# One VectorE instruction for the tails of two groups, with the fold ahead of it, in a compressed interaction network on one Trainium2 core

## The reference

```
h = inputs                                             # (512, 40, 32)
for i, (W, bias) in enumerate(params):                 # three layers, 200 outputs each
    x = einsum('bhd,bmd->bhmd', h, inputs)             # all pairs of h and the 40 fields
    y = relu(einsum('oi,bid->bod', W, x.reshape(B, -1, D)) + bias)
    if i != 2:  h, direct = split(y, 2, axis=1)        # 100 feed the next layer, 100 are output
    else:       direct = y
    outs.append(direct)
z = concatenate(outs, axis=1).sum(-1)                  # then three dense layers
```

## Time and profile before

| | before |
|---|---|
| median of 3 runs | 2834.54 us (2829.89 to 2837.47) |
| the profiled execution's own time | 2834.67 us |
| its span, first to last instruction | 2832.9 us |
| TensorE busy | 2777.7 us (98%) |
| VectorE busy | 2637.5 us (93%) |
| ScalarE busy | 1501.3 us (53%) |
| GpSimd busy | 845.0 us (30%) |
| mean granted TensorE clock | 0.996 of full |

### The profile page before, as it was taken

The page is one execution under the profiler, slowest core; times in us unless marked ns, Lnnn a source line. Parts: engine busy times, 40 slices in busy tenths (PEclk is TensorE's granted clock), DMA queues, the critical chain, the costliest instruction groups (busy, mean ns, idle before and its releaser), DMA issues.

```text
span 2832.9 us, 53974 instructions
## 1 busy us (share of the span) xinstructions
PE 2777.7 (98%) x18996; PEld 2759.8 (97%) x18996; DVE 2637.5 (93%) x1945; ACT 1501.3 (53%) x1880; POOL 845.0 (30%) x698
## 2 busy tenths in 40 slices
PE   4999999999999999999999999999999999999999
PEld 3999999999999999999999999999999999999997
DVE  5899999999999999999999999999999999999994
ACT  3555555555555555555555555555555555555553
POOL 4432332332332332333333323323323323323100
PEclk9999999999999999999999999999999999999999
DMA  7433433433433333333333334334334334334320
GB/s 196 97 77 78 96 90 75 100 87 76 102 83 80 98 85 82 96 85 84 94 84 88 92 81 93 90 77 96 89 76 98 89 76 101 87 76 102 91 62 18
DMA packets 286069, 249.65 MB, mean 88 GB/s; under 512 B 31247, under 2 KB 284527, under 8 KB 285938
## 3 DMA queue, kind: packets, MB, share of 16 engines
q1 hardware_dynamic: 209462, 195.99, 24.6%
q0 software_dynamic: 65616, 45.43, 12.1%
q10 hardware_dynamic: 10962, 7.87, 1.0%
HBM read 140.74 MB, written 4.20 MB: 51 GB/s over the span
## 4 chain that ended last, share of the span: by engine, by line
PE 93%; DVE 2%; issue 2%; DMA 1%; POOL 1%; SPq 1%; ACT 0%; another core or an unknown queue 0%; ACTq 0%; DVEq 0%
PE acc L805 61%; PE acc L807 28%; PE hid_ps L818 1%; PE z_ps L822 1%; DVE tails L717 1%; POOL gathered L429 1%; DVE product L712 1%; SPq L366 1%; PE acc L868 0%; DMA acc_copy<-acc_copy 0%; DMA raw_weights<-in_w 0%; PE hid_ps L891 0%; DMA gathered<-in_table,rows_all 0%; DVE weights L672 0%; DVE product L710 0%
## 5 line engine op out<-in xcount | busy, mean ns | idle before, releaser
L805 PE MATMUL acc<-weights,heads 126*128 126x400 f32 (+1 forms) x9088 | 2698.8, 365 | 49.6 <-issue 28.8
L807 PE MATMUL acc<-weights,tails 126*128 126x200 f32 (+1 forms) x9088 | 2323.5, 256 | 0.0
L805 PEld LDWEIGHTS acc<-weights,heads 126*128 126x128 f32 (+1 forms) x9088 | 1715.1, 189 | 53.3 <-issue 37.2
L516 ACT ACTIVATE heads<-product 126x1024 fp32r<-126x1024 f32 (+2 forms) x1152 | 1198.6, 1048 | 1037.3 <-PE acc L807 516.8
L807 PEld LDWEIGHTS acc<-weights,tails 126*128 126x128 f32 (+1 forms) x9088 | 1743.2, 192 | 0.0
L717 DVE TENSOR_TENSOR tails<-product,heads 126x1024 fp32r<-126x1024 f32 (+2 forms) x1152 | 1349.2, 1204 | 2.6 <-ACT heads L516 2.6
L712 DVE TENSOR_TENSOR product<-hid_rep,x_rep 126x2048 f32<-126x2048 f32 x510 | 1167.6, 2289 | 107.4 <-PE acc L807 65.6
L437 POOL DMA_DIRECT2D acc_copy<-acc_copy x189 | 236.3, 1250 | 1742.6 <-ACT acc_copy L522 1741.0
L429 POOL DMA_INDIRECT gathered<-in_table,rows_all x320 | 497.4, 1554 | 100.9 <-issue 96.9
L530 ACT ACTIVATE y_relu<-acc_copy 128x400 f32<-128x400 f32 x192 | 102.3, 533 | 210.3 <-DMA acc_copy<-acc_copy 204.9
L522 ACT ACTIVATE acc_copy<-acc 128x800 f32<-128x800 f32 x192 | 158.8, 827 | 16.1 <-PE acc L807 14.0
(11 more groups left out here) (23 smaller groups left out, 85.7 us busy)
## 6 DMA issues: line engine op xcount, KB each, us to landing
x_rep<-x_rows SPq DMA_DIRECT2D x512, 120.0 KB
hid_rep<-hid SPq DMA_DIRECT2D x511, 120.0 KB
x_pairs<-x_rows SPq DMA_DIRECT2D x191, 280.0 KB
acc_copy<-acc_copy POOLq DMA_DIRECT2D x189, 200.0 KB
hid_rep<-hid SPq DMA_DIRECT2D x511, 5.0 KB
x_pairs<-x_rows SPq DMA_DIRECT2D x63, 120.0 KB
raw_weights<-in_w ACTq DMA_DIRECT2D x12, 500.0 KB, 8.0
gathered<-in_table,rows_all POOLq DMA_INDIRECT x320
```

Source lines behind the costliest of these rows:

```text
L516: act.activation(heads[0:rows, ring % HEADS_RING, 0:tiles, :], product[0:rows, ring % PRODUCT_RING, 0:tiles, :], ACT.Copy).then_inc(heads_ ...
L805: nc.tensor.matmul(acc[:, at.parity, c, 0:2 * LAYER], dims(heads[0:rows, ring % HEADS_RING, k, :], c), w, start=(q == 0 and k == 0), stop= ...
L807: last = nc.tensor.matmul(acc[:, at.parity, c, LAYER:2 * LAYER], dims(tails[0:rows, ring % PRODUCT_RING, k, :], c), w[:, 0:LAYER], start=F ...
```

## The change

The tails of a pair of groups become one instruction of 2048 columns (1792 for layer 0), which waits until both heads are made and then reports both groups at once. A fold that stood between the two tails now stands ahead of the one instruction.

```
-            def make_tails(layer, q, g, ring):
-                tiles, rows = group_tiles(layer, q), OPERAND_ROWS[layer]
-                dve.wait_ge(heads_made, g + 1)
-                dve.tensor_tensor(tails[0:rows, ring % PRODUCT_RING, 0:tiles, :],
-                                  product[0:rows, ring % PRODUCT_RING, 0:tiles, :],
-                                  heads[0:rows, ring % HEADS_RING, 0:tiles, :].bitcast(F32),
-                                  ALU.subtract).then_inc(tails_made, 1)
+            def make_tails(layer, g, ring):
+                tiles, rows = TILES0 if layer == 0 else 2 * GROUP, OPERAND_ROWS[layer]
+                pair = slice(ring % PRODUCT_RING, ring % PRODUCT_RING + 2)
+                heads_pair = slice(ring % HEADS_RING, ring % HEADS_RING + 2)
+
+                def flat(x):
+                    return x.rearrange("p a b c -> p (a b) c")[:, 0:tiles, :]
+
+                dve.wait_ge(heads_made, g + 2)
+                dve.tensor_tensor(flat(tails[0:rows, pair, :, :]), flat(product[0:rows, pair, :, :]),
+                                  flat(heads[0:rows, heads_pair, :, :]).bitcast(F32),
+                                  ALU.subtract).then_inc(tails_made, 2)
...
             def make_previous_tails(g, ring, between=None):
 
-                layer, q = previous[0]
-                make_tails(layer, q, g - 2, (ring - 2) % RING)
+                layer = previous[0][0]
                 if between:
                     fold(*between)
-                make_tails(layer, q + 1, g - 1, (ring - 1) % RING)
+                make_tails(layer, g - 2, (ring - 2) % RING)
                 previous[0] = None
```

## The result

The changed kernel takes 2984.93 us (median; 2982.38 to 2989.24), the one before, run beside it, 2835.89: a ratio of 1.0529 (95% interval 1.0514 to 1.0545), 149 us slower. The prediction was 3016 us, in a range of 2950 to 3055: the direction held, the size was 31 us too large, and of the three costs that the prediction added up two came about; the third, the late fold of layer 2, did not. The span is 2982.4 us.

A forecast was written before the change was run, and what follows sets the result against it. TensorE was taken to set the time, VectorE just ahead of it. A turn of 45.63 us against 42.79 gave 170 us over sixty turns, plus 12 for the others: 2834.67 + 182, rounded to 3016 us, range 2950 to 3055.

The forecast's parts named there:

- three costs: The pair loop's stalls, the fold ahead at (1,2) and the fold ahead at (2,4); 2.84 us a turn with restarts.
- the late fold of layer 2: At (1,2): fold waits for a relu ending at 7.69; (1,2) starts at 10.35, with (1,0)'s stall 1.54 us together.
- The loop of 4.83 us against 4.70: VectorE's way round a pair, 0.27 + 2.21 + 2.29 + 0.06 us, exceeds TensorE's time for a pair by 0.13.
- stall at (2,2): (2,2) to (2,4)'s predecessor pair: the plain loop takes 4.83 us against 4.69, 0.14 more.
- The fold of layer 1 ahead of (2,4): Fold waits for its relu, so (2,4) starts 10.72 us after (2,0) against 9.72: 1.00 more.
- (1,4) to stay unstalled: From (1,4) to (1,6), VectorE needs 9.1 us, TensorE's two pairs take 10.10: no stall, only 0.09 of restart.
- The sum: A turn of 45.63 us against 42.79, 2.84 more; 170 us for sixty turns, 12 for others, giving 3016.
- The outer turns: Five turns outside the hardware loop (1, 2, 3, 64, 65): 12 us counted, between 0 and 28.
- The pair loop alone: Rival, chance 0.07: folds wait little as transfers land earlier in longer turns; 1.16 us a turn, 2907 us.
- the 1.6 that the rival had charged to each turn: Clock rival, chance 0.04: TensorE's stalls halve its clock for 3.2 us each turn, some 100 us more, 3116.
- VectorE's saving: Rival "Faster", chance 0.03: if VectorE set the time, fewer, longer instructions would save 31 us: 2803.
- What I said the profile would show: Signs: TensorE waits for tails some 110 us, nearly 190 times; turn 45.6; tails 2.29; 0.7 idle before folds.

The follow-up runs named there:

- E1: The changed kernel with both folds behind the pair's single tails instruction instead of ahead of it: 2918.15 us, ratio 1.0285.
- E3: The changed kernel with a pair's products in two instructions, each waiting only for its own group's place in the ring: 2976.53 us, ratio 1.0492.
- E4: E3 with both folds behind the tails, which stay one instruction: 2854.14 us, ratio 1.0058.
- E7: The changed kernel with a pair's products in two instructions, with the single wait of before ahead of both: 2998.85 us, ratio 1.0573.
- E9: The changed kernel with only the fold of layer 1 behind the tails, that of layer 2 still ahead: 2936.57 us, ratio 1.0367.
- E6: The changed kernel with SyncE's eight hid_rep transfers for layer 2 issued later in the loop, by a later wait: 3021.38 us, ratio 1.0647.
- E2: The kernel before, two tails a pair, with the fold ahead of both tails: 2878.17 us, ratio 1.0137.
- E5: The kernel before, two tails a pair, with both folds behind the two tails: 2843.75 us, ratio 1.0031.

## Why the prediction was right, and where it was off

The direction and two of the three costs came about by the mechanism forecast; the fold of layer 2, which the prediction called the larger term of its two, cost next to nothing in the loop. In a turn 0.73 us too much at (1,2) met 0.25 too little at (1,4) and (2,4), so the time came nearer than the parts were.

- **The loop of 4.83 us against 4.70.** Measured 4.82 at (1,0), (1,4) and (2,0). (1,2) and (2,2) came at 4.80 and 4.79, but TensorE wasn't stopped there: the 0.09 are the restart before. So the 0.14 forecast as a stall at (2,2) was no stall; the loop's start, set at 0.27 us behind TensorE's start of a pair, hangs on the end of the group before, which a stop doesn't delay. E1 shows it without the folds, E3 and E4 remove it by letting the first product start earlier, E7 shows that this permission and not the splitting did it.
- **The fold of layer 1 ahead of (2,4).** Predicted: (2,4) 10.72 us after (2,0). Measured 10.84. Its relu ended 8.29 us after (2,0), and 8.33 before; with the fold behind the tails (E1, E9) (2,4) comes at 9.97, 0.87 earlier.
- **The fold of layer 2 ahead of (1,2): the step that was mis-sized.** It said that the relu ends at 7.69 and that "the change doesn't bring it forward", and further down "No transfer is moved". The term was 10.35 us from (0,0) to (1,2); it measured 9.62. SyncE's waits count VectorE's products, so against a TensorE that starts (0,0) late its transfers began 1.2 us earlier; the add had less beside it (2 packets in place of 103), and the relu ended at 6.82, while the fold's turn on VectorE came at 6.94. E6 shows cause and size: the transfers moved back by 1.05 us bring 7.54, 10.29 and 36 us.
- **(1,4) to stay unstalled.** Predicted 4.69 and the restart; measured 4.82. It hung on the same step: only with a late fold at (1,2) would TensorE have come later and the products behind it found their permission earlier. In E6, where it is late, the place shows 4.79, which is the restart alone.
- **The sum.** 2.84 us a turn were predicted, 170 for the loop; it was 134.6. The outer turns were taken at 12 us and measured 14.8.
- **Rivals.** The pair loop alone (2907) is E1, 2918: it exists but is not the change. Its reason, that the transfers land earlier in longer turns, is what happened to the fold of layer 2 and not to that of layer 1. The clock's mean was 0.994 (0.996 before). In the sixty turns it fell once, to half for 3.4 us at 2423.7, behind a wait of TensorE of 1.86 us; (2,4) to (2,6) took 6.38 us there in place of 4.81, near the 1.6 that the rival had charged to each turn. VectorE's saving of 25.7 us bought nothing: start to start, with the overlap of the two tails, it was only 0.07 us a pair (2.27 to 2.20: 1665.63 to 1667.83), and of busy time 0.152 (2284 ns against two of 1218). By the rule of the Trainium skill ("VectorE: DVE Perf Modes", on the TRN2 errata) an estimate is 0.157 us saved a pair. The trace agrees with it on busy time.
- **What I said the profile would show.** Tails of 2.29: yes. A turn of 45.6: 45.1. Waits of TensorE for tails of some 110 us: 133.2, of which the first wait is 30.8, so 102; but 121 times and not 190: the profile shows two waits a turn, at (1,0) and (2,4), and no third at (1,2). Idle before both folds: only before that of layer 1.

## What to carry to other kernels

When two engines run in lockstep through a ring, compare the way round (permission to start, work, work, signal) with the time that the consumer takes from giving the permission to needing that work (here one pair, 4.70 us), and not the busy shares: here an instruction that saved 0.07 us a pair also delivered its first half 1.07 us later, and the slack was 1.0. Small work that waits for something on a side path belongs behind what the engine that sets the time needs next, and ahead of its own reader; E2 and E5 show what missing either edge costs. And when a change makes that engine later, everything that is started by counts of the other engines moves against it, the transfers too: predict their new places before you reuse an old landing time.

## What the runs showed of the hardware

A restart of TensorE costs 0.09 us after a wait of any length seen in the loop (up to 1.86 us): the first matmul takes 0.45 to 0.47 in place of 0.36. Waits of 0.5 to 1.1 us, two a turn of 45 us, left the granted clock at full. In the changed kernel's sixty turns 15 waits were longer, 1.10 to 1.86 us, and only behind the longest of them did the clock fall, to half for 3.4 us.

GpSimd's indirect gathers, all the same 320 of them, took 1554 ns on average before and 1906 in the changed kernel, with values from 1548 (E3) to 1940 (E5) in the others. E5 has no long tails, so their length isn't the cause; what is stays open. The distances above don't follow it: E5 with 1940 ns has a turn of 43.04 us, E3 with 1548 one of 44.90.

The time from the end of the accumulator's copy to the relu of layer 2, most of it the adding transfer, moved between 5.03 us (before), 4.51 (E1) and 4.29 (changed kernel) as other transfers moved, with 5.01 in E6 again.
